# Second attention of a macaron network: the norm steps of its first and last head stand at other places in each engine's order

## What is computed

```python
x = x + 0.5 * _L1_ffn_ref(_layernorm(x, axis=-1), L1_ffn_gate_w, ...)
x = x + _L1_attn_ref(_layernorm(x, axis=-1), L1_attn_Wq, L1_attn_Wk, L1_attn_Wv, L1_attn_Wo)
x = x + 0.5 * _L1_ffn_ref(_layernorm(x, axis=-1), L1_ffn_gate_w, ...)

# _L1_attn_ref: 16 heads of width 128
q, k, v = x @ Wq.T, x @ Wk.T, x @ Wv.T
q, k = _apply_rope(q, cos, sin), _apply_rope(k, cos, sin)
scores = where(causal, einsum('bthd,bshd->bhts', q, k) * scale, -inf)
y = einsum('bhts,bshd->bthd', softmax(scores), v)
return y / 3.0 @ Wo.T
```

## Time and profile before

| | before |
|---|---|
| median of 3 runs | 1787.68 us (1786.37 to 1788.04) |
| the profiled execution, its own time | 1790.02 us |
| its span on the core | 1788.2 us |
| TensorE matmul busy | 1673.8 us (94%) |
| VectorE busy | 1380.6 us (77%) |
| ScalarE busy | 1246.9 us (70%) |
| GpSimd busy | 1081.2 us (60%) |
| `Attention1` in the span | from about 476 us to about 1688 us |

### The profile page before, as it was taken

How to read it: one execution, slowest core, us unless ns; L and a number is a source line. 1 busy time by engine, 2 the same in 40 slices (tenths; PEclk the granted TensorE clock), 3 DMA queues, 4 the chain that set the end, 5 groups by cost and what they waited for, 6 DMA issues and landing times.

```text
span 1788.2 us, 37269 instructions
## 1 busy us (share of the span) xinstructions
PE 1673.8 (94%) x11566; PEld 1440.7 (81%) x11566; DVE 1380.6 (77%) x3611; ACT 1246.9 (70%) x3255; POOL 1081.2 (60%) x1098
## 2 busy tenths in 40 slices
PE   6998988999789999999999999999999999999899
PEld 4777876778778788888888878878888887887788
DVE  7358865475698898988989889898888988989453
ACT  4335642345378879779788897887978888788742
POOL 2633114553247767767685786776778678677732
PEclk9999999999999999999999999999999999999999
DMA  8843047640048867786696876868779587786700
GB/s 294 242 79 48 13 163 230 150 100 1 15 79 149 127 119 136 119 145 122 117 157 97 153 124 121 138 118 136 131 120 152 100 145 125 119 142 121 134 21 28
DMA packets 636133, 215.96 MB, mean 121 GB/s; under 512 B 587296, under 2 KB 622752, under 8 KB 635808
## 3 DMA queue, kind: packets, MB, share of 16 engines
q1 hardware_dynamic: 625568, 200.71, 58.3%
q0 software_dynamic: 10368, 12.85, 4.4%
HBM read 51.06 MB, written 19.80 MB: 40 GB/s over the span
## 4 chain that ended last, share of the span: by engine, by line
PE 60%; DVE 17%; ACT 8%; issue 7%; DMA 4%; POOL 3%; SPq 0%; ACTq 0%; POOLq 0%; DVEq 0%
PE phase_scores L1277 16%; PE phase_y L166 6%; PE phase_y L168 6%; PE phase_y L167 6%; ACT phase_p L1311 4%; PE phase_ring L166 4%; PE phase_ring L168 4%; PE phase_ring L167 4%; DVE phase_peaks L1290 2%; DVE phase_ring L2628 2%; PE phase_up_ps L166 2%; DMA y_rows<-phase_out,phase_rows 2%; DVE phase_crossed L2626 2%; DVE phase_crossed L2625 2%; PE phase_up_ps L168 2%
## 5 line engine op out<-in xcount | busy, mean ns | idle before, releaser
L2336 POOL TENSOR_TENSOR phase_split<-phase_p,phase_split 128x512 f16<-128x512 f32 (+3 forms) x640 | 650.4, 1016 | 183.1 <-ACT phase_split L2305 139.3
L1311 ACT ACTIVATE phase_p<-phase_scores,phase_bias 128x512 f32<-128x512 f32 (+3 forms) x680 | 417.7, 627 | 75.8 <-DVE phase_bias L2331 52.9
L2305 ACT ACTIVATE phase_split<-phase_p 128x512 f16<-128x512 f32 (+3 forms) x640 | 338.7, 578 | 4.8 <-DMA phase_pt<-phase_split 3.3
L1290 DVE TENSOR_REDUCE phase_peaks<-phase_scores 128x1 f32<-128x512 f32 (+1 forms) x408 | 267.1, 668 | 69.1 <-PE phase_scores L1277 66.3
L166 PE MATMUL phase_y<-phase_pt,phase_v_hi 128*128 128x256 f16 (+1 forms) x1152 | 308.0, 269 | 2.7 <-DMA phase_pt<-phase_split 2.0
L167 PE MATMUL phase_y<-phase_pt,phase_v_hi 128*128 128x256 f16 (+1 forms) x1152 | 307.6, 267 | 0.0
L168 PE MATMUL phase_y<-phase_pt,phase_v_lo 128*128 128x256 f16 (+1 forms) x1152 | 304.2, 267 | 0.0
L1277 PE MATMUL phase_scores<-phase_k_hi,phase_q_hi 128*128 128x512 f32 (+3 forms) x640 | 255.4, 399 | 38.4 <-ACT phase_p L1311 25.7
L2705 POOL TENSOR_TENSOR sb_x<-sb_x,phase_part 128x512 f32<-128x512 f32 x128 | 164.0, 1282 | 127.4 <-ACT phase_part L2562 121.7
L1277 PE MATMUL phase_scores<-phase_k_hi,phase_q_lo 128*128 128x512 f32 (+3 forms) x640 | 233.1, 364 | 0.0
L1277 PE MATMUL phase_scores<-phase_k_lo,phase_q_hi 128*128 128x512 f32 (+3 forms) x640 | 233.0, 364 | 0.0
(11 more groups left out here) (313 smaller groups left out, 4485.8 us busy)
## 6 DMA issues: line engine op xcount, KB each, us to landing
phase_pt<-phase_split SPq DMA_TRANSPOSE x640, 3.3
y_rows<-phase_zero SPq DMA_DIRECT2D x16, 512.0 KB, 7.6
phase_e_up<-expert_up SPq DMA_DIRECT2D x16, 352.0 KB, 4.2
phase_e_dn<-expert_down SPq DMA_DIRECT2D x16, 256.0 KB, 5.4
xn_rows<-phase_ln_xn SPq DMA_DIRECT2D x8, 512.0 KB, 2.9
sb_x<-y_rows POOLq DMA_DIRECT2D x8, 512.0 KB, 6.2
late_raw_qk<-qk SPq DMA_DIRECT2D x16, 256.0 KB, 3.2
phase_logits_t<-expert_up SPq DMA_DIRECT2D x8, 352.0 KB, 4.2
```

The costliest lines, as they stand in the source:

```text
L1290: dve.tensor_reduce(peak, scores, AX.X, ALU.max).then_inc(*self.peaked.one)
L1311: act.activation(self.p_room(act, key)[:, 0:width], self.scores[:, at:at + width], ACT.Exp, bias=self.bias[:, t % 2:t % 2 + 1], accum_out= ...
L2305: act.activation(hi, value, ACT.Copy).then_inc(*self.t_hi.one)
L2336: pool.tensor_tensor(lo, value, hi, ALU.subtract).then_inc(*self.t_lo.one)
```

## The change

`with_norms` no longer works the places out from anchors in its code; it reads them from a table, `PLACES`, which has for each engine pairs of a step and of what is put behind it. The steps and what they compute are the same, as many as before; the order of all other steps is the same too, and SP's order is unchanged. The core of the diff (the table has 30 such entries in all):

```diff
+PLACES = {
+    "pe": ((("project", 0, 3), ("flip", 3, 0)),
+           (("values", 0, 0), ("flip", 3, 1)),
+           (("score", -1, 15, 3), ("next_flip", 0, 0), ("next_flip", 0, 1)),
...
+    "dve": ((("bound", 0), ("stats", 3)),
+           (("finish", 0, 0), ("scale", 3)),
...
+           (("score", -1, 11, 0), ("next_stats", 0)),
...
     def with_norms(self, engine, order):
 
-        def after(anchor, *steps):
-            if anchor in order:
-                order[order.index(anchor) + 1:order.index(anchor) + 1] = steps
...
+        for after, *steps in PLACES[engine]:
+            at = order.index((after[0], after[1] % NH, *after[2:])) + 1 if after else 0
+            order[at:at] = steps
         return order
```

More of the change, by code:

```diff
@@ L2096 @@
 }
+PLACES = {
+    "pe": ((("project", 0, 3), ("flip", 3, 0)),
+           (("values", 0, 0), ("flip", 3, 1)),
+           (("score", -1, 15, 3), ("next_flip", 0, 0), ("next_flip", 0, 1)),
+           (("out", -1, 5), ("next_flip", 1, 0)),
+           (("pv", -1, 6, 0), ("next_flip", 1, 1)),),
+    "act": ((("finish", 0, 1), ("scale", 3)),
+           (("turn", 0, 0, 0), ("flip", 3, 0)),
+           (("finish", 0, 4), ("flip", 3, 1)),
+           (("turn", -1, 12, 0), ("next_scale", 0)),
+           (("turn", -1, 14, 0), ("next_flip", 0, 0)),
+           (("turn", -1, 14, 2), ("next_flip", 0, 1)),
+           (("round", -1, 5), ("next_scale", 1)),
+           (("turn", -1, 15, 1), ("next_flip", 1, 0)),
+           (("round", -1, 6), ("ahead", 0), ("ahead", 1)),
+           (("out", -1, 7), ("next_flip", 1, 1)),),
+    "dve": ((("bound", 0), ("stats", 3)),
+           (("finish", 0, 0), ("scale", 3)),
+           (("score", 0, 6, 0), ("flip", 3, 0)),
+           (("invert", 0, 6), ("flip", 3, 1)),
+           (("score", -1, 11, 0), ("next_stats", 0)),
+           (("invert", -1, 13), ("next_scale", 0)),
+           (("score", -1, 14, 3), ("next_stats", 1)),
+           (("score", -1, 15, 0), ("next_flip", 0, 0)),
+           (("score", -1, 15, 3), ("next_flip", 0, 1), ("next_scale", 1)),
+           (("round", -1, 5), ("next_flip", 1, 0)),
+           (("round", -1, 6), ("ahead", 0)),
+           (("round", -1, 7), ("ahead", 1), ("next_flip", 1, 1)),),
+    "pool": ((("bound", 0), ("stats", 3)),
+           (("turn", -1, 10, 2), ("next_stats", 0)),
+           (("turn", -1, 13, 2), ("next_stats", 1)),),
+    "sp": (),
+}
 AHEAD = (0, 1)
```

30 lines of the change are left out of this document (removed).

## The result

| | before | after |
|---|---|---|
| median of the runs made side by side, us | 1786.55 (5 runs, 1786.37 to 1788.04) | 1796.80 (5 runs, 1795.81 to 1797.72) |
| profiled execution, us (span) | 1790.02 (1788.2) | 1797.16 (1795.3) |
| from the memset of ones to `gated1`'s first matmul, us | 1211.45 | 1221.92 |

A forecast was written before the change was run, and what follows sets the result against it. TensorE was taken to set the pace in mid-attention, chains of waits through VectorE at the start. Terms -1.1 + 4.7 + 0.3 + 3.0 - 0.9 + 0.8 = 6.8 us on 1787.68 gave 1794.5 us, range 1789.5 to 1798.5.

The forecast's parts named there:

- Start: First head, stats 3 behind bound 0: TensorE's 7.31 us idle ahead of the first score becomes 5.9; minus 1.1 us.
- Statistics 0: Head 15, next_stats 0 ahead of finish 15,6: VectorE waits for GpSimd's addition, delaying score 15,12,0; plus 4.7 us.
- Clock: After 4.4 us idle in head 15 TensorE runs at 1.2 GHz, making project 15,7 late; plus 0.8 us.
- Scale 0: Head 15, next_scale 0 ahead of the bias of tile 14: score 15,15,0 waits for it; plus 0.3 us.
- Flip 0,0: Head 15, next_flip 0,0 among the scores of tile 15: VectorE's wait delays that tile's bias; plus 3.0 us.
- End: TensorE's eight transposes between out 15,6 and out 15,7 move into waiting time, so gated1 starts sooner; minus 0.9 us.
- Rival 1: TensorE's later idle times, 5.5 us in all, are slack and absorb the waits: 1787.7 us; chance 12%.
- Rival 2: Head 15's wait for GpSimd's addition is absent, only the 1.75 us of statistics count: 1789.9 us; chance 8%.
- Rival 3: Less idle time at the start keeps TensorE at 2.4 GHz; with waits absorbed too, 1784.6 us; chance 4%.
- the edge: Lowest edge of the forecast's band (1791.3 to 1798.2 us), counted under no change, which was given 0.19.

The follow-up runs named there:

- e12: The kernel before the change with only stats 3 moved behind bound 0, on VectorE and GpSimd; ratio to before 0.9991.
- e3: The changed kernel with next_stats 0 (VectorE, GpSimd) and ScalarE's next_scale 0 moved back to their old places; ratio to before 1.0010.
- e4: The changed kernel with only VectorE's half of next_flip 0,0 moved back behind score 15,15,3; ratio to before 1.0034.
- e5: The changed kernel with next_flip 0,0 and 0,1 moved back behind the last scores on TensorE, ScalarE and VectorE; ratio to before 1.0041.
- e2: The changed kernel with the steps of chunk 3 (start) as before, so only the last head is changed; ratio to before 1.0056.

## Why the prediction was right, and where its terms were off

The direction, the mechanism and the range (1789.5 to 1798.5) held; the size was too small. The forecast was 1794.5 us, the measured median 1796.80. The distance between the medians is 10.25 us where 6.8 were forecast; the two differ less in the absolute time because before's median beside the change was 1786.55 and not 1787.68. In the stage it is +10.5 against +6.8. By the prediction's own terms:

- **Start, -1.1.** The idle time of 5.9 us came out at 5.92, and e12 confirms -1.4 for the power of the bound. In the profiled execution of after only -0.37 were left at tile 9, outside the ends (-1.4 and -0.7), and +0.54 at head 15: 1.6 us worse than forecast. The term left the clock out. The eleven profiles with the new start stood at -2.4 to +0.8 in head 15, and they part where the granted clock does, in the first head and in the heads between.
- **Statistics 0, +4.7.** Measured 4.70 at tile 11, with VectorE idle for 3.01 (3.1 forecast) and TensorE for 4.20 (4.4). e3 shows that it all comes from this step.
- **Clock, +0.8.** Measured 1.89 us between tiles 11 and 13 in after, 1.95 in e4 and 2.18 in e5, but 0.79 in e2, all with the same order of steps in this place. TensorE stood at 0.50 for 5.3, 5.4 and 5.9 us behind the idle time there, and for 2.9 in e2. So the term goes with the length of the slow stretch, which differs from profile to profile; VectorE waited for project 15,7 1.60 us in after and 1.06 in e2. They lie about within the ends 0 and 2; the 0.8 fits one of the four profiles and is too small for three.
- **Scale 0, +0.3.** Measured +1.70 at tile 14 and 0.80 us given back behind it, +0.9 together, within the ends (-0.7 and 1.0). Of the 1.70, 1.02 are VectorE's: the step from the first score of tile 14 to its bias grew from 4.17 to 5.19 us, with the pair 1.09 us long. The 0.80 are what I had as the 0.7 us that could be given back: from the bias of tile 14 to score 15,15,0 it takes 1.11 us, not 1.91, since the bias comes so late that ScalarE has done its splits and stands waiting for it, in e3 as well. What I left out is ScalarE's half at its new place: next_scale 0 now stands among the splits of tile 12, and the exponential of tile 13 starts 0.84 us after its bias, not 0.19. That is the other 0.7 us; in e3, where ScalarE's half stands at its old place, it is gone:

```profile
1657.71 1.14 ACT L315 ACTIVATE phase_xn<-sb_x,phase_ln_shift,phase_ln_rstd 128x256 f32<-128x256 f32 x2
...
1659.94 0.72 ACT L1311 ACTIVATE phase_p<-phase_scores,phase_bias 128x512 f32<-128x512 f32 x1
```

- **Flip 0,0, +3.0.** Right for the bias of tile 15: 3.13 us more between the last score and it (4.80 against 1.67), and 3.13 come back in e4. With the 0.80 us from above this makes the +2.32 of the table. But moving the flips back does not return all of it at the end: 1.66 to 2.18 us in e4 and e5. Chunk 1's statistics, which stand at this place too and have no term, cost nothing at the bias of tile 15 in e4 and e5.
- **End, -0.9.** Measured -0.68. VectorE's ahead 1 has moved too, behind round 15,7, which the table of places leaves out; no run takes the two apart.

The start (+1.6), the clock (+1.1), the scale (+0.6), the end (+0.2) and the flips (+0.1) make up the 3.7 us. More than two thirds of it are start and clock, and go with how long TensorE stayed at 0.50 in this one profile. The medians moved by as much (10.25 us); where the executions without a profile lost it is not on record. Rival 1 (absorbed) fell: behind the first wait only the place ahead of score 15,15,0 gave something back, 0.8 us, and the 2.04 us at the last chunk were filled, not won. Rival 2 fell: VectorE's idle was 3.01 us. Rival 3 fell: after 5.92 us of idle time the first score's matmul still took 0.47 us, as in the earlier trace rows. A weak form of it is seen all the same: from the first score on TensorE stood at 0.50 for 6.1 us in before and for 3.3 to 5.3 us in nine of the eleven profiles with the new start, though for 6.4 in after.

Three slips in the working change nothing: the lower ends add up to +3.5, not +3.6; rivals 1 and 2 and the edge are more than 0.19, since the rivals alone have 0.20; and the bias of tile 15 came 1.67 us after the last score matmul in before by the earlier trace rows, not 1.5, so that the forecast for it was 4.7, and 4.80 was measured.

The Trainium skill's rule, page "SBUF — State Buffer", section "Who interferes with whom" (a VectorE tensor_scalar in a two-port mode and a GpSimd instruction shut each other out), agrees with what the runs show. The pair of L305 took 0.73 us with no split or addition of GpSimd beside it, in the first head and in head 15 alike, and 1.09 to 2.55 us as next_scale 0 beside them, and each of its slow instructions ended 0.15 us after one of GpSimd's. Four BATCH_NORM_STATS2, which also run beside the splits, took 1.39 to 1.41 us wherever they stood. The prediction said that by this rule its sum would be 0.7 us higher; in after the pair was only 1.09 us long, as it began 0.2 us ahead of the end of an addition. That the pair runs in such a mode no run here tests.

## What to carry to other kernels

On an engine that works its instructions in order, the price of a step moved ahead is the time at which its input is ready minus the time at which the engine gets there, plus its own work, and it is charged to whatever is queued behind it: the step itself did not become urgent by standing early. An idle time of the engine further on can take a part of it, and a clock that falls behind the wait adds to it (here 0.8 to 2.2 us behind 4.20 us of idle time). Before moving a step, find for each of its halves, on every engine, the chain that the next instruction belongs to; an idle time on the pacing engine that ends with a chain through those engines is no slack. And look instead at what stands in a critical run without belonging to it: two additions moved out of GpSimd's last splits brought 1.84 us, and no norm step moved ahead at the end of the stage brought as much. When the differences are of this size, read the granted clock beside every shift before giving it a cause.
